# Two attention stages: TensorE turns a unit's weights ahead of the values product of the unit before it

## The chip, the cores and the metric

The program runs on one core of a Trainium2 chip. The metric is the device time of that core in microseconds, from the first to the last instruction of one launch. Three timed executions of the kernel before are given, and one more execution was taken with the hardware profiler; every row below comes from that one.

## The reference, cut to what matters

The model is a chain of six layers on a batch of 64 sequences of 128 tokens of width 128, all in fp32. Two of the six have attention with 16 heads of width 8. Only these two are touched by the change.

```python
# layer L0_xattn: cross attention, 77 context tokens, masked
scores = jnp.einsum('nhqd,nhkd->nhqk', q, k)
scores = jnp.where(mask == 0, jnp.float32(-1000000000.0), scores)
attn = jax.nn.softmax(scores / math.sqrt(dk), axis=-1)
out = jnp.einsum('nhqk,nhkd->nhqd', attn, v)
return out.transpose(0, 2, 1, 3).reshape(n, qlen, h * dk) @ wo.T + bo
...
# layer L1_xattn, first half: self attention that keeps the u = 5 largest scores of each row
scores = jnp.einsum('bhqd,bhkd->bhqk', q, k) * (1.0 / math.sqrt(D))
_, idx = jax.lax.top_k(scores, u)
...
# layer L1_xattn, second half: cross attention over the 77 context tokens, no mask, then a feed-forward part
x_cross = _mha_cross(x, memory, cross_in_w, cross_in_b, cross_out_w, cross_out_b)
h = jax.nn.gelu(x @ ffn_w1.T + ffn_b1, approximate=False)
```

## The kernel before, in words

Six stages run one after the other. The stage of L0_xattn (tiles `xa_...`) and the stage of L1_xattn (tiles `de_...`, "the decoder") share one class, `Attend`. Both work in rounds over groups of four sequences; there are 16 groups, and the rounds of different groups are laid over each other like a pipeline, so there are 19 rounds, of which the first and the last ones are partly empty. A round is one block of code for each engine, and all engines meet at a barrier between rounds.

Inside a round the attention is cut into **units**: one unit is 8 of the 16 heads of one sequence, so a sequence is two units. The xattn stage has 8 units in a round, all of the masked kind that needs no search. The decoder has 16: steps 0 to 7 are self-attention units with a search for the largest scores (`topk`), steps 8 to 15 are cross-attention units without one (`whole(t)` is true for these).

Each engine walks through the steps t = 0, 1, 2, ... of the round in its own fixed order, and semaphores tie the orders together. For a unit t without a search the chain is:

1. TensorE `pe_scores` (L1011, and L1015 for the mask) in step t-2, into banks 0 and 1.
2. VectorE `dve_shift` (L1154, L1157) in step t-1: row maximum, and scores minus maximum, into `e`.
3. ScalarE `act_exp` (L1094) in step t.
4. TensorE `pe_turn` (L1026) in step t: 8 transposes of `e` into banks 4 and 5.
5. ScalarE `act_turned` (L1100) in step t+1: copies banks 4 and 5 into `pt`.
6. TensorE `pe_values` (L1037) in step t+1: weights times values into bank 6, for the 8 heads.
7. After the second unit of a sequence: ScalarE `act_values` (L1106) copies bank 6 into `ot`, TensorE `pe_back` (L1045) turns it, VectorE `dve_normalise` (L1163, L1166) divides, TensorE `pe_out` (L1050), ScalarE `act_out` (L1111) copies into `ots`, TensorE `pe_project` (L1054), VectorE `dve_add`.

Banks 4 and 5 exist once. So `pe_turn` of unit t waits for `pt` of unit t-1, which is the same signal that `pe_values` of unit t-1 waits for:

```python
def pe_turn(self, pe, t):
    self.wait(pe, "pick" if self.topk(t) else "exp", t)
    self.wait(pe, "pt", t - 1)
...
def pe_values(self, pe, t):
    self.wait(pe, "pt", t)
```

ScalarE's order inside step t is fixed by `act_step`: `act_exp(t)`; in even steps `act_out`, which waits for `pe_out`, the last thing TensorE did in step t-1; then `act_turned(t-1)`; in even steps `act_values`, which waits for `pe_values(t-1)`, the last values product of a sequence. After `act_step` the stage adds its own work to some steps: in the xattn stage two activations after step 1, one after step 2, one after step 3, and after step 4 the query bias (L1380) and four rows of a layer norm (L881 into `xa_z`), after step 5 four more rows (into `xa_y_tok`). In the decoder, after step 8, the last two bias activations of the feed-forward part (L2358) and the Gelu (L2362, with a table load), on which TensorE's second feed-forward product (L2323) waits; that product stands between steps 8 and 9 of TensorE. After step 10 stand four rows of a layer norm (L881 into `de_xn`), which wait for GpSimd, and a copy (L2153).

Of the kernel before, what the change touches and what calls it, by code (L numbers as in the profile page):

```python
# [915 lines left out]
class Attend:  # L916
# [139 lines left out]
    def pe_step(self, pe, t):  # L1056
        there, early = self.unit(t + 2) is not None, not self.whole(t + 1)
        if there and early:
            self.pe_scores(pe, t + 2)
        if self.unit(t - 1) is not None:  # L1060
            self.pe_values(pe, t - 1)
        if t % 2 == 0 and self.unit(t - 4) is not None:
            self.pe_project(pe, (t - 4) // 2)
        if self.unit(t) is not None:
            self.pe_turn(pe, t)
        if there and not early:
            self.pe_scores(pe, t + 2)
        if t % 2 == 0 and self.unit(t - 2) is not None:
            self.pe_back(pe, (t - 2) // 2)
        if t % 2 == 1 and self.unit(t - 3) is not None:  # L1070
            self.pe_out(pe, (t - 3) // 2)
# [1755 lines left out]
```

## Time and profile before

| | us |
|---|---|
| timed executions | 8492.16, 8483.58, 8464.30 |
| median of them | 8483.58 |
| the profiled execution, its own time | 8499.55 |
| its span, first to last instruction | 8497.5 |
| xattn stage, attention at work | about 4240 to 4930 |
| decoder stage | about 6370 to 8110 |

The span and the execution's own time differ by 2 us, which lie outside of the instructions. The two stages of the change take 2430 us of the 8497. "Granted clock" is the share of full speed that TensorE was given over a stretch; at any moment it is either 2.4 GHz (1.00) or 1.2 GHz (0.50), so 0.90 over a stretch means that a fifth of it ran at the lower level.

### The profile page before, as it was taken

The numbers are of one execution on the slowest core, as the hardware profiler recorded it, in microseconds if no ns is written. First come the engines' busy times: TensorE is split into PE (matmuls) and PEld (weight loads), VectorE is DVE, ScalarE is ACT, GpSimd is POOL, SyncE is SP. The second block draws the span as 40 slices with busy tenths as digits, with TensorE's granted clock in tenths as the row PEclk, the third lists the DMA queues.
The fourth block names the chain that finished last, engine by engine and source line by source line (L and its number), as shares of the span: only waits on it lengthen the run. The fifth ranks groups of instructions, "written<-read, shape, count | busy, mean of one in ns | idle before, by whom it ended". The sixth has DMA issues, their size and how long they took to land. (4 is left out here: it accounts for less than half of the span.)

```text
span 8497.5 us, 93901 instructions
## 1 busy us (share of the span) xinstructions
PE 6487.2 (76%) x25844; PEld 3454.5 (41%) x25859; DVE 6694.5 (79%) x15635; ACT 4390.8 (52%) x8810; POOL 4876.1 (57%) x2829
## 2 busy tenths in 40 slices
PE   5888888888888888888788867777556777777745
PEld 2333333333333333333355545555434545555532
DVE  5999999999999999999755558888667666666657
ACT  3555555555555555555455523333226666666633
POOL 4888878888888878888644434444222333333310
PEclk8898889899898899898898978888658988888855
DMA  5333333334333333333300046767310000000011
GB/s 184 133 148 155 137 149 155 132 148 160 133 148 155 132 153 151 137 148 155 112 25 22 20 132 204 208 201 206 92 47 7 10 9 9 9 9 9 6 31 36
DMA packets 373728, 896.56 MB, mean 106 GB/s; under 512 B 28031, under 2 KB 270076, under 8 KB 306972
## 3 DMA queue, kind: packets, MB, share of 16 engines
q1 hardware_dynamic: 332508, 692.64, 21.7%
q0 software_dynamic: 40960, 201.36, 8.3%
q14 instruction: 208, 1.70, 0.1%
q8 instruction: 52, 0.85, 0.0%
HBM read 850.58 MB, written 56.77 MB: 107 GB/s over the span
## 5 line engine op out<-in xcount | busy, mean ns | idle before, releaser
L380 POOL TENSOR_TENSOR mb_dBu<-mb_dtu,mb_rows_b 128x1024 f32<-128x1024 f32 x1027 | 2405.7, 2359 | 363.3 <-DVE mb_bank L394 186.6
L394 DVE TENSOR_TENSOR_SCAN mb_bank<-mb_bank,mb_dBu 128x1024 f32<-128x1024 f32 x704 | 1612.8, 2291 | 72.0 <-PEq L63 50.9
L434 PE MATMUL mb_bank<-mb_hcd,ident 128*128 128x512 f32 x2560 | 1271.6, 624 | 78.9 <-DVE mb_hcd L408 78.8
L365 ACT ACTIVATE mb_bank<-mb_dt,mb_a_neg 128x508 f32<-128x508 f32 x2050 | 1315.1, 673 | 0.8
L434 PE MATMUL mb_bank<-mb_hcp,ident 128*128 128x512 f32 x1280 | 796.7, 755 | 355.0 <-POOL mb_hcp L417 355.0
L417 POOL TENSOR_TENSOR mb_hcp<-mb_hs,mb_rows_c 128x1024 f32<-128x1024 f32 x320 | 752.8, 2352 | 360.0 <-DVE mb_hs L394 359.7
L408 DVE TENSOR_TENSOR mb_hcd<-mb_bank,mb_rows_c 128x1024 f32<-128x1024 f32 x704 | 862.1, 1225 | 31.3
L434 PEld LDWEIGHTS mb_bank<-mb_hcd,ident 128*128 128x128 f32 x2560 | 502.1, 203 | 798.3 <-issue 591.3
L1537 POOL DMA_INDIRECT ex_rows<-in_ex_table,ex_idx x512 | 490.3, 958 | 561.3 <-DVE ex_idx L1533 331.9
L394 DVE TENSOR_TENSOR_SCAN mb_hs<-mb_bank,mb_dBu 128x1024 f32<-128x1024 f32 x320 | 730.9, 2284 | 42.2 <-ACT mb_bank L365 42.2
L434 PEld LDWEIGHTS mb_bank<-mb_hcp,ident 128*128 128x128 f32 x1280 | 284.8, 236 | 806.1 <-POOL mb_hcp L417 480.1
L362 ACT ACTIVATE mb_bank<-mb_zeros 128x8 f32<-128x8 f32 x1025 | 175.9, 172 | 725.9 <-DVE mb_hcd L408 351.2
L207 PE MATMUL mb_bank<-mb_h_ch,mb_w_conv 128*128 128x512 f32 x1040 | 493.7, 618 | 0.0
L1026 PE MATMUL de_bank<-ident,de_a_e 128*128 128x128 f32 (+1 forms) x2048 | 332.6, 315 | 202.3 <-DVE de_a_e L1146 202.3
L996 POOL TENSOR_TENSOR de_a_km<-de_xT,hmask 128x2048 f32<-128x2048 f32 x64 | 231.8, 3622 | 394.1 <-PE de_bank L1011 252.5
L996 POOL TENSOR_TENSOR de_a_km<-de_kT,hmask 128x1232 f32<-128x1232 f32 x64 | 157.6, 2462 | 523.0 <-PE de_bank L1011 523.0
L1026 PEld LDWEIGHTS de_bank<-ident,de_a_e 128*128 128x128 f32 (+1 forms) x2048 | 270.2, 166 | 247.5 <-DVE de_a_e L1146 226.1
L996 POOL TENSOR_TENSOR xa_a_km<-xa_kT,hmask 128x1232 f32<-128x1232 f32 x64 | 144.5, 2258 | 360.8 <-PE xa_bank L1015 262.8
L1131 DVE MAX8 de_a_m<-de_a_sp 128x8 f32<-128x128 f32 x1024 | 210.3, 280 | 154.5 <-ACT de_a_sp L1080 96.1
L1089 ACT ACTIVATE de_a_e<-de_a_sp,de_a_nb 128x128 f32<-128x128 f32 x1024 | 314.4, 402 | 32.5 <-PEq L63 32.5
L207 PEld LDWEIGHTS mb_bank<-mb_h_ch,mb_w_conv 128*128 128x128 f32 x1040 | 211.2, 203 | 281.1 <-issue 281.1
L1591 PE MATMUL ex_bank<-ex_rows,ex_dg_in 128*128 128x256 f32 x1024 | 322.7, 486 | 0.0
(369 smaller groups left out, 13327.9 us busy)
## 6 DMA issues: line engine op xcount, KB each, us to landing
mb_rows_b<-bc_rows SPq DMA_DIRECT2D x259, 1024.0 KB, 7.6
mb_rows_c<-bc_rows SPq DMA_DIRECT2D x258, 1024.0 KB, 6.8
stream<-mb_r_post SPq DMA_DIRECT2D x69, 256.0 KB, 2.4
mb_r_tok<-stream SPq DMA_DIRECT2D x67, 256.0 KB, 2.8
mb_r_post<-stream SPq DMA_DIRECT2D x65, 256.0 KB, 2.9
ex_rows<-in_ex_table,ex_idx POOLq DMA_INDIRECT x512
tj_x_tok<-stream SPq DMA_DIRECT2D x17, 256.0 KB, 3.0
bc_rows<-mb_xp SPq DMA_DIRECT2D x65, 64.0 KB, 1.6
```

The lines of the kernel that those rows point to most:

```text
L207: m = nc.tensor.matmul(bank[:, M0 + c], w_conv[:, k, c * P:(c + 1) * P], h_ch[:, :, k:k + SEQ], start=(k == 0), stop=(k == DC - 1))
L365: e = nc.scalar.activation(da_of(n)[:, c * GB:(c + 1) * GB, 1:], dt[q][:, c].rearrange("p (b t) -> p b t", b=GB)[:, :, 1:], ACT.Exp, scale ...
L380: nc.gpsimd.tensor_tensor(by_c(dBu[m % RING][:]), by_c(chains(dtu[q][:])), over_c(rows_b[:, n]), ALU.mult).then_inc(s["mb_dbu"], 1)
L394: nc.vector.tensor_tensor_scan(flat(to), flat(da_of(n)), flat(dBu[n % RING][:]), 0.0, ALU.mult, ALU.add).then_inc(s["mb_scan"], 1)
L408: nc.vector.tensor_tensor(by_c(hcd[k % 3][:]), by_c(da_of(n)), over_c(rows_c[:, n]), ALU.mult).then_inc(s["mb_hcd"], 1)
L417: nc.gpsimd.tensor_tensor(by_c(hcp[k % 2][:]), by_c(hs[k % 2][:]), over_c(rows_c[:, n]), ALU.mult).then_inc(s["mb_hcp"], 1)
L434: m = nc.tensor.matmul(bank[:, B_Y + c], ident[:], part[:, c * GB:(c + 1) * GB], start=False, stop=False)
L996: self.nc.gpsimd.tensor_tensor(self.km[n % 2][:, :, 0:nk], kind.k(n % GB).unsqueeze(1).to_broadcast([P, H, nk]), self.hmask[:].unsqueeze(2 ...
L1026: m = self.nc.tensor.transpose(self.bank[0:nk, 4 + h // 4, (h % 4) * P:(h % 4 + 1) * P], self.e_of(t, nk)[:, h], self.ident[:])
L1089: m = self.nc.scalar.activation(self.e_of(t, nk)[:, h], self.sp[t % 2][:, h, 0:nk], ACT.Exp, scale=kind.scale, bias=self.nb[:, t % 2, h:h ...
L1537: nc.gpsimd.indirect_dma_start(rowsb[b][:, h], None, w["table"], bass.IndirectOffsetOnAxis(idx[b][:, h:h + 1], 0)).then_inc(got[b], 16)
L1591: m = nc.tensor.matmul(bank[:, HID, 0:FI], dg_in[:, h], rowsb[k % GB][:, h, IB:IB + FI], start=False, stop=(h == PH - 1))
```

## The change

In `pe_step`, TensorE's order within a step, a unit without a search is turned before the values product of the unit behind it. Units with a search keep the old order. No instruction is added or removed.

```diff
         there, early = self.unit(t + 2) is not None, not self.whole(t + 1)
         if there and early:
             self.pe_scores(pe, t + 2)
+        if self.whole(t):
+            self.pe_turn(pe, t)
         if self.unit(t - 1) is not None:
             self.pe_values(pe, t - 1)
         if t % 2 == 0 and self.unit(t - 4) is not None:
             self.pe_project(pe, (t - 4) // 2)
-        if self.unit(t) is not None:
+        if self.topk(t):
             self.pe_turn(pe, t)
         if there and not early:
             self.pe_scores(pe, t + 2)
```

## Rows read from the trace of the kernel before

**Rows 1.** Stages: length, busy PE, PEld, DVE, ACT, POOL (instructions), granted clock, DMA share, GB/s.
```profile
4240.00:4930.00 690.00, 604.11 (x4540) 375.08 (x4539) 374.87 (x1169) 350.18 (x614) 272.67 (x219) 0.89 0.08 21
6370.00:8110.00 1740.00, 1273.47 (x9089) 865.17 (x9087) 1157.03 (x4988) 1096.45 (x2232) 617.65 (x385) 0.85 0.03 9
```

**Rows 2.** TensorE's waits in each stage: us in total, times, longest.
```profile
PE xa_bank L1037 <- ACT xa_a_pt L1100: 85.6, 62, 2.8
...
PE de_bank L1037 <- ACT de_a_pt L1100: 168.0, 143, 3.7
PE de_bank L2323 <- ACT de_hT L2362: 34.7, 15, 2.3
```

**Rows 3.** TensorE in order of time, xattn, steps 4 to 6 of a round.
```profile
4655.44 0.64 PE L1037 MATMUL xa_bank<-xa_a_pt,xa_vx 77*32 77x128 f32 x16
4656.01 0.49 PE L1054 MATMUL xa_bank<-xa_wo,xa_a_ots 128*128 128x128 f32 x2
4656.34 1.04 PE L1026 MATMUL xa_bank<-ident,xa_a_e 128*77 128x128 f32 x8
4657.21 0.68 PE L1011 MATMUL xa_bank<-xa_a_km,xa_qT 128*128 128x308 f32 x2
...
4660.43 0.64 PE L1037 MATMUL xa_bank<-xa_a_pt,xa_vx 77*32 77x128 f32 x16 [0.76 <-ACT xa_a_pt L1100]
...
4665.44 0.64 PE L1037 MATMUL xa_bank<-xa_a_pt,xa_vx 77*32 77x128 f32 x16 [1.37 <-ACT xa_a_pt L1100]
...
4669.60 0.64 PE L1037 MATMUL xa_bank<-xa_a_pt,xa_vx 77*32 77x128 f32 x16
```

**Rows 4.** ScalarE in order of time, the same round, steps 4 to 7.
```profile
4656.15 0.60 ACT L1106 ACTIVATE xa_a_ot<-xa_bank 128x512 f32<-128x512 f32 x1 [1.15 <-PE xa_bank L1037]
...
4657.21 1.65 ACT L881 ACTIVATE xa_z<-xa_r_tok,xa_n_shift,xa_n_rstd 128x128 f32<-128x128 f32 x4
...
4659.36 1.01 ACT L1100 ACTIVATE xa_a_pt<-xa_bank 77x1024 f32<-77x1024 f32 x1
...
4664.11 0.28 ACT L1111 ACTIVATE xa_a_ots<-xa_bank 128x128 f32<-128x128 f32 x1 [1.58 <-PE xa_bank L1050]
4664.29 1.01 ACT L1100 ACTIVATE xa_a_pt<-xa_bank 77x1024 f32<-77x1024 f32 x1
4666.14 0.60 ACT L1106 ACTIVATE xa_a_ot<-xa_bank 128x512 f32<-128x512 f32 x1 [0.84 <-PE xa_bank L1037]
...
4667.41 1.02 ACT L1100 ACTIVATE xa_a_pt<-xa_bank 77x1024 f32<-77x1024 f32 x1
```

**Rows 5.** TensorE, decoder, steps 8 and 9 of a round.
```profile
7134.94 0.64 PE L1037 MATMUL de_bank<-de_a_pt,de_vself 128*32 128x128 f32 x16
7135.84 1.04 PE L1026 MATMUL de_bank<-ident,de_a_e 128*77 128x128 f32 x8
...
7140.69 5.47 PE L2323 MATMUL de_bank<-de_w,de_hT 128*128 128x128 f32 x32 [2.33 <-ACT de_hT L2362]
```

**Rows 6.** ScalarE, decoder, the same step 8, and step 10.
```profile
7135.65 0.60 ACT L1106 ACTIVATE de_a_ot<-de_bank 128x512 f32<-128x512 f32 x1 [1.13 <-PE de_bank L1037]
...
7152.44 1.66 ACT L881 ACTIVATE de_xn<-de_a,de_n_shift,de_n_rstd 128x128 f32<-128x128 f32 x4 [0.95 <-POOL de_n_shift L875]
```

**Rows 7.** The same turn and values at the lower clock, xattn, TensorE.
```profile
4616.38 1.08 PE L1037 MATMUL xa_bank<-xa_a_pt,xa_vx 77*32 77x128 f32 x16 [1.37 <-ACT xa_a_pt L1100]
4617.98 1.91 PE L1026 MATMUL xa_bank<-ident,xa_a_e 128*77 128x128 f32 x8
```

**Rows 8.** Busy time by engine over two whole rounds of each stage, xattn first.
```profile
4605.42:4654.48 49.06, 43.35 (x290) 26.72 (x289) 24.50 (x78) 22.58 (x41) 18.43 (x16) 0.79 0.08 22
4654.48:4694.05 39.57, 34.17 (x291) 21.31 (x289) 24.10 (x78) 22.59 (x41) 18.44 (x16) 1.00 0.11 28
...
6607.04:6712.72 105.68, 77.42 (x572) 53.06 (x573) 72.52 (x314) 69.31 (x142) 39.78 (x25) 0.90 0.03 10
7140.69:7249.94 109.25, 81.16 (x573) 55.40 (x573) 72.09 (x314) 69.20 (x142) 39.74 (x25) 0.84 0.03 9
```

## The prediction

> **What bounds the kernel now.** I began with the busy time by engine in the two stages that the change touches [rows 1]. In the xattn stage TensorE is busy for 604 of 690 us, no other engine for more than 375: TensorE sets the pace, and only the 86 us in which it stands idle can be won. In the decoder it is busy for 1273 of 1740 us and VectorE for 1157; which of them waits changes within a round. Together the stages are 2430 us, so one per cent of them is 0.3% of the kernel.
>
> Next I read TensorE's waits [rows 2]. In the xattn stage one line holds practically all of the idle time: the values product (L1037) waiting for ScalarE's copy of the turned weights (L1100), 85.6 us in 62 waits. The decoder has the same wait (168 us, partly in units with a search) and one for the Gelu (L2323 waiting for L2362), 15 times 2.3 us.
>
> Then I laid TensorE's and ScalarE's order of time side by side for a few steps [rows 3, 4], to see who is late behind the copy. In step 5 TensorE waits 0.76 us and in step 6 1.37 us. In step 6 ScalarE had first to copy `ots` at 4664.11, for which it had waited 1.58 us for `pe_out` (L1050), the last thing that TensorE does in step 5; only then came the turned weights, at 4664.29. So the wait of step 6 is a round trip through `pe_out`, and the turned weights had been ready long before. In step 5 ScalarE never waited for the turn either: from `ot` at 4656.15 it ran without a gap through the query bias, four rows of the norm, the exponent and the copy, to 4660.37, and what it had waited for ahead of that (1.15 us) was the values product. The reader is to see that ScalarE's queue, not the turn, is what makes the copy late.
>
> **The change part by part.** Nothing is removed or added; one group of 8 transposes trades places with one group of 8 values products (and the projection behind it in even steps). I take the effects one by one.
>
> *The wait ahead of the pair.* Turn t and values t-1 wait for the same copy, since banks 4 and 5 exist once. The exponent of unit t stands ahead of that copy in ScalarE's order, so the turn finds it done. The pair starts when it started before: 0.
>
> *The turn ends earlier*, by the values product (4655.44 to 4656.01, 0.57 us) and in even steps the projection (0.33 us) [rows 3]. Who can use that? Only the copy of unit t. For odd t it stands behind `act_out`, which waits for the end of TensorE's step, so nothing is won. For even t it stands behind `act_values`, which waits for the values product of unit t-1; this is the very one that now comes later. So nothing is won there either. VectorE's `shift` of unit t+2 also waits for the turn, but its turn comes a step later, so it has cover. Gain: 0; the upper bound is the rival below.
>
> *The values product ends later*, by the turn: 4656.34 to 4657.21, 0.87 us at the full clock [rows 3]. Behind `act_values` ScalarE holds everything else, so the question is for each even step how much cover there is before TensorE needs what comes next.
> - Xattn, step 6: `ot` at 4666.14, the copy ends at 4668.43 and TensorE comes for it at 4669.60 [rows 3, 4]. Cover 1.17 us, need 0.87: hidden. In steps 0 and 2 TensorE has the next group's transposes besides, so the cover should be no smaller: hidden.
> - Xattn, step 4: no cover at all, since the chain runs without a gap to TensorE's 0.76 us wait. It becomes 1.63. `act_step` is in step 4 followed by both extra pieces in the rounds that have a next group and a norm two ahead, 14 of them. 14 x 0.87 = 12.2 us. TensorE's remaining steps of the round depend on ScalarE only through `pe_out`, so the delay reaches the end of the round whole.
> - Decoder, step 8: values product at 7134.94, `ot` at 7135.65 after a wait of 1.13, and behind it in ScalarE's queue two bias activations, a table load and the Gelu, on which TensorE waits 2.33 us until 7140.69 [rows 5, 6]. Again no cover. The turn there takes the same 0.87. Fifteen rounds have this wait [rows 2]: 15 x 0.87 = 13.1 us.
> - Decoder, step 10: behind `ot` ScalarE waits 0.95 us for GpSimd [rows 6], which swallows 0.87. Steps 12 and 14 have no wait of TensorE on this chain; there ScalarE also waits for other things. 0, at most 0.87 for one of them in each of 15 rounds, 13 us.
> - `pe_back` waits for `ot` but stands at the end of the same step, behind four scores products. `dve_add` waits for the projection, now 0.87 later, ahead of the `shift` that TensorE's next scores need; that `shift` has a step of slack. 0.
>
> At the lower clock the turn takes nearly twice as long (1.91 against 1.04 us busy) [rows 7], but so does everything with which TensorE covers ScalarE, whose own work does not stretch; step 4 then has cover. So the price per place lies between 0 and 0.87, or 1.6 if only the turn is slow; I take 0.87, as the step 4 and step 8 rows are at the full clock.
>
> Sum: 12.2 + 13.1 = 25.3 us more. The profiled execution took 8499.55 us, which would become 8524.9. It lies 16 us above the median of the three timed ones, 8483.58, and on that the sum gives 8508.9. I predict 8509.
>
> **The clock.** A whole xattn round took 49.06 us at a granted clock of 0.79 and the next one, with the same instructions, 39.57 us at 1.00; a decoder round took 105.68 us at 0.90 and a later one 109.25 at 0.84 [rows 8]. So the clock moves a round by far more than the 0.87 us of the change, and adding idle time of TensorE may tip it in either direction. This is the largest unknown of the forecast, and the reason for most of the range.
>
> The Trainium skill (page TensorE: Matmul & The Clock Gate, section Part 1: The HAM clock gate) says that the throttled state is the default and that activity releases it. No row here contradicts this, but the two xattn rounds differ by 9.5 us with nearly equal idle time (5.7 and 5.4 us), so the amount of idle alone does not decide it here. By that rule the added idle should cost clock, which is the second rival below, at 8537; by the rows alone the sum is 8509.
>
> **The rivals.**
> - *The delays arrive as computed*: 8509, with a range of its own of 8495 to 8523, from the scatter of the three times. Chance 0.42.
> - *More time at the lower clock.* The longer idle of steps 5 (1.63 us, followed by 1.37) and 9 (3.2 us) is followed by more work at 1.2 GHz. Price: if half of the 14 xattn rounds lose the half of the difference between the two rows of [rows 8] less often seen now, say 4 rounds x 4.7 = 19 us, and the three decoder rounds or so that still are of the short kind lose 3.6 us each, 11 us; with some of it overlapping, 28 us on top, 8537. It decides against the first case from about one xattn round in seven. Chance 0.17.
> - *The clock swallows the delays.* The rounds of the decoder repeat with one length; if they keep it, the 13.1 us vanish, and with half of the xattn part the time is 8490. It also stands for cover that I did not see. Chance 0.20.
> - *Less time at the lower clock.* A moved phase lets the decoder's long rounds become the short kind: 12 x 3.6 = 43 us less, against 25 more: 8466. It ends on the other side from 8 such rounds on. Chance 0.13.
> - *The early turn does what it says*: the waits of L1037 shrink by the values product, because ScalarE's copy is bound by the turn after all. Three such waits in each of 14 + 15 rounds, 0.57 each, 50 us less: 8434. Against it speaks the order in ScalarE's queue [rows 4]. Chance 0.08.
>
> **How the numbers follow.** About 0.3% or 25 us is what a measurement of this kernel can tell from no change. The first case lies on that bound, so I give half of it to each side. Slower by over 0.3%: 0.21 + 0.16 = 0.37. Within: 0.21 + 0.19 + 0.06 = 0.46. Faster: 0.07 + 0.08 + 0.02 = 0.17. The range leaves out the last rival and the extreme of the second: 8465 to 8545.
>
> **What would show it.** In the profile after: in 14 xattn rounds the wait ahead of step 5 grows from 0.76 to about 1.6, and now stands at L1026 instead of L1037; the wait ahead of step 6 stays 1.37; the decoder's L2323 waits 3.2 instead of 2.33; ScalarE's wait ahead of L1106 grows by 0.87 everywhere, while its wait ahead of L1100 hardly moves. A full-clock xattn round takes 40.4 instead of 39.57 us. The prediction is wrong if the 1.37 us waits shrink (then the turn was on the path), if the 0.76 does not grow (then ScalarE's chain had cover), or if the number of rounds at each clock moves the total by more than the 25 us.

## The result, and the profile after

The changed kernel takes 8607.61 us (median of 5 runs, 8599.93 to 8623.65), the kernel before 8481.15 (median of 5). The ratio is 1.0156 with a 95% interval of 1.0143 to 1.0169: 126 us slower, where 25 were forecast, and outside the range of 8465 to 8545.

The waits of TensorE in the profile after, xattn stage first (us in total, times, longest), beside [rows 2]:

```profile
PE xa_bank L1026 <- ACT xa_a_pt L1102: 101.4, 62, 2.9
...
PE de_bank L2325 <- ACT de_hT L2364: 46.8, 15, 3.2
```

The number of waits is the same, 62 and 15. The first group grew from 85.6 to 101.4 us, the second from 34.7 to 46.8. That is 15.8 and 12.1 us, 28 together, against the 12.2 and 13.1 of the forecast. In order of time TensorE goes through steps 4 to 6 of a round of the xattn stage like this, at the full clock:

```profile
4612.44 1.04 PE L1026 MATMUL xa_bank<-ident,xa_a_e 128*77 128x128 f32 x8
4613.40 0.64 PE L1037 MATMUL xa_bank<-xa_a_pt,xa_vx 77*32 77x128 f32 x16
...
4618.48 1.07 PE L1026 MATMUL xa_bank<-ident,xa_a_e 128*77 128x128 f32 x8 [1.71 <-ACT xa_a_pt L1102]
...
4623.65 1.07 PE L1026 MATMUL xa_bank<-ident,xa_a_e 128*77 128x128 f32 x8 [1.36 <-ACT xa_a_pt L1102]
```

The reader is to compare with [rows 3]: the wait ahead of step 5 is 1.71 us instead of 0.76, the one ahead of step 6 1.36 instead of 1.37, and both now stand at the turn. ScalarE in the same steps, beside [rows 4]:

```profile
4614.12 0.60 ACT L1108 ACTIVATE xa_a_ot<-xa_bank 128x512 f32<-128x512 f32 x1 [2.03 <-PE xa_bank L1037]
...
4622.32 0.28 ACT L1113 ACTIVATE xa_a_ots<-xa_bank 128x128 f32<-128x128 f32 x1 [1.85 <-PE xa_bank L1050]
```

It waits 2.03 us for the values product where it waited 1.15, which is the turn's 0.87. So far everything went as predicted. Where is the rest? In the busy time. Both stages again, with the changed kernel's longer windows (columns as in [rows 1]):

```profile
4240.00:5020.00 780.00, 677.50 (x4515) 413.21 (x4515) 373.83 (x1169) 345.19 (x614) 271.65 (x219) 0.80 0.07 19
6460.00:8230.00 1770.00, 1294.51 (x9078) 866.88 (x9076) 1149.05 (x4993) 1089.95 (x2231) 617.71 (x386) 0.86 0.03 9
```

The xattn stage takes 780 us instead of 690. TensorE is busy for 677.5 us with the same instructions that took 604.1 before: 73 us more, beside 16 us more of waiting, make up the 90. The granted clock of the stage fell from 0.89 to 0.80. VectorE's and ScalarE's busy times did not grow. In the decoder the busy time grew by 21 us and the Gelu wait by 12, in a stretch 30 us longer, although the mean clock over it did not fall (0.86 after 0.85); so its 21 us can't be put down to clock from these rows. The comparison of rounds, beside [rows 8]:

```profile
4657.22:4710.52 53.30, 46.47 (x290) 28.17 (x289) 24.37 (x78) 22.30 (x41) 18.36 (x16) 0.74 0.08 21
4710.52:4756.19 45.67, 39.14 (x290) 24.31 (x289) 24.04 (x78) 22.30 (x41) 18.36 (x16) 0.89 0.10 24
...
7143.57:7252.74 109.17, 80.50 (x573) 54.21 (x573) 71.68 (x314) 68.86 (x142) 39.73 (x25) 0.87 0.03 9
```

Before, rounds of 39.57 us at 1.00 came up again and again; after, the rounds at the highest clock are like the second row here, 45.67 us at 0.89. A decoder round of 105.7 us, as the first rounds before had it, was not found after: all 13 full rounds come at about 109.2, as the third row shows, where the trace before has nine of that length.

### The profile page after: what moved, and what is told of

It reads as the page before. It is cut to its first block and busy times, and to the rows that moved or that the text cites. A ratio compares the mean times of both kernels' runs of the same rounds, so it can differ in the third digit from the quotient of the medians.

```text
span 8621.7 us, 93901 instructions
## 1 busy us (share of the span) xinstructions
PE 6572.9 (76%) x25844; PEld 3488.8 (40%) x25859; DVE 6683.1 (78%) x15635; ACT 4370.9 (51%) x8810; POOL 4870.4 (56%) x2829
```

## The experiments

All medians are compared with executions of the kernel before on the same chip, whose own median moved between 8460.92 and 8476.83 us from group to group. I give the ratio with its interval; the us are differences of medians. Each kernel has one trace. For the xattn stage I quote the row of the stretch from 4300 to 4850 us, which lies inside the stage in every kernel; for the two orders it reads, before and after:

```profile
4300.00:4850.00 550.00, 478.88 (x3618) 296.21 (x3620) 303.85 (x961) 284.69 (x504) 232.79 (x189) 0.90 0.09 24
```

```profile
4300.00:4850.00 550.00, 476.61 (x3142) 290.48 (x3141) 265.67 (x844) 244.01 (x438) 201.18 (x165) 0.79 0.08 22
```

In the same time TensorE is busy equally long and gets through 13% fewer instructions.

The edits of the first kernels are one condition. `per` is 4 in the xattn stage and 8 in the decoder:

```diff
+        first = self.whole(t) and (CONDITION)
+        if first:
+            self.pe_turn(pe, t)
         if self.unit(t - 1) is not None:
             self.pe_values(pe, t - 1)
         if t % 2 == 0 and self.unit(t - 4) is not None:
             self.pe_project(pe, (t - 4) // 2)
-        if self.unit(t) is not None:
+        if self.unit(t) is not None and not first:
             self.pe_turn(pe, t)
```

**The two stages apart.** Condition `self.per == 4`:

> The new order in the xattn stage alone. The changed kernel lost 126 us by the medians; in the two profiles the xattn stage accounts for about 92 to 96 us of the 124 us of span. Both theories below expect 85 to 105 us more than the kernel before here, and 14 waits of 1.71 us ahead of step 5. If the loss is spread differently (a lost clock that carries over from stage to stage), it is clearly less or more than that.

8575.35 us against 8473.52, ratio 1.0119 (1.0102 to 1.0136), 102 us. As expected.

Condition `self.per == 8`:

> The new order in the decoder alone: 15 waits of 3.20 us for the Gelu in place of 2.33 (13 us). Expected 15 to 35 us more than before; decoder rounds stay at 109.2 us in most rounds, as in both profiles. Together with the xattn-only kernel it should make up the 126 us.

8516.74 us against 8473.52, ratio 1.0045 (1.0030 to 1.0059), 43 us, above the expected 35. The sum of the two is 145, a little more than the 126 of both.

**Is it the added idle?** Condition `self.per == 4 and t == 4`:

> Xattn stage, new order in step 4 alone: this adds all of the idle time of the change (0.76 to about 1.7 us ahead of step 5, 14 times), but no transposes stand directly behind a wait, since step 4 itself begins without one. Theory A (the added idle tips the clock): most of the 90 us, 60 to 100. Theory B (the turn directly behind a wait tips the clock, whatever the length of the wait): 12 us of idle and little else, 5 to 30.

8490.07 us, ratio 1.0018 (1.0006 to 1.0030), 17 us. This kernel has the whole added wait and the new order in no other step, and it costs what the sum had said within its interval. Theory A falls. The added wait is not quite free of clock, though: the stage's granted clock is 0.87, and in the trace the stage grew by 24 us, counted from the first query product (out of `xa_wq`, one in each round) to the last: 668.4 after 644.5.

Condition `self.per == 4 and t != 4`:

> Xattn stage, new order in every step but 4: the wait ahead of step 5 stays 0.76 to 0.85 us, so no idle time is added, but turns stand directly behind the waits of steps 0, 2, 5 and 6. Theory A: 0 to 15 us more than before and a granted clock of 0.89 in the stage. Theory B: 60 to 90 us more and a granted clock near 0.80.

8526.30 us, ratio 1.0053 (1.0033 to 1.0074), 53 us, with no longer wait ahead of step 5. The clock is 0.85. Theory B is nearer, but 17 and 53 make 70 of the 102 us.

**Which steps?** Condition `self.per == 4 and t in (1, 3, 7)`, the steps without a wait:

> Xattn stage, new order in steps 1, 3 and 7 alone, where TensorE comes to the pair without a wait. Theory B3 (it matters whether the turn or the values product stands directly behind a wait): 0 to 8 us more than before, rounds of 39.6 us and longer ones mixed as before. If it costs 25 us or more, the place behind a wait is not what matters in the kernel with every step but 4 (53 us more).

8495.64 us against 8476.83, ratio 1.0023 (1.0011 to 1.0034), 19 us; more than the 8 that I allowed, less than 25. The clock is 0.89 after 0.90.

Condition `self.per == 4 and t in (0, 2, 5, 6)`, the steps that begin with one:

> Xattn stage, new order in steps 0, 2, 5 and 6 alone, each of which begins with a wait; the length of the waits changes by less than 0.15 us. Theory B3: 35 to 60 us more than before, rounds near 46 us and none of 39.6. Theory C (a matter of the rounds' phase against the clock alone): anything between -20 and +60.

8558.85 us, ratio 1.0108 (1.0075 to 1.0141), 82 us by the medians. This was more than expected, and almost the loss of the whole change in this stage. Its waits and its stage row:

```profile
PE xa_bank L1026 <- ACT xa_a_pt L1103: 65.2, 45, 2.9
```

```profile
4300.00:4850.00 550.00, 486.04 (x3201) 293.61 (x3202) 270.02 (x853) 247.54 (x444) 205.40 (x168) 0.79 0.08 22
```

45 waits of 1.45 us in the mean; the kernel before has, over the same stretch, 51 waits of 1.39 us. So the length of the waits is the same, the work is the same, and the clock is 0.79 instead of 0.90. Only the order of turn and values product behind the wait differs.

This kernel also spoils the simple account that the turn behind a wait is what costs. The kernel above with every step but 4 is this one with the new order in steps 1, 3 and 7 on top. Those steps alone cost 19 us, so it should cost about 100; it costs 53, and the intervals of the two kernels (1.0033 to 1.0074, 1.0075 to 1.0141) do not meet. In the traces this kernel settles at rounds of about 51.1 us, and the one with more of the new order in it at 46.0:

```profile
4679.69:4730.78 51.09, 45.43 (x291) 27.30 (x289) 24.54 (x78) 22.30 (x41) 18.38 (x16) 0.77 0.08 22
```

```profile
4673.87:4719.89 46.02, 40.36 (x290) 24.91 (x289) 24.26 (x78) 22.30 (x41) 18.35 (x16) 0.85 0.10 24
```

So the cost is not a property of a step that can be added up.

**Work put into the waits.** If idle time of TensorE is what lets the clock fall, filling it must bring the clock back, whatever the order. The fill goes into columns of bank 6 that a later values product overwrites, ahead of the waits of steps 0, 2, 5 and 6:

```diff
+    def fill():
+        for k in range(2):
+            nc.tensor.matmul(bank[:, 6, 384:512], ident[:], ident[:], start=True, stop=True)
...
     for t in range(8):
+        if t in (0, 2, 5, 6) and has_now and (t or has_ended):
+            fill()
         at.pe_step(pe, t)
```

> New order in the xattn stage alone (102 us more than before without a fill), plus two ordinary 128x128 products of the unit matrix with itself, about 0.65 us at the full clock, into unused columns of bank 6 ahead of the waits of steps 0, 2, 5 and 6; they fit inside the waits and their values are never read. Theory B1 (the clock follows TensorE's work other than turns): the stage gets most of its clock back, 0 to 50 us more than before. Theory B2 (any TensorE work counts alike): the same here, so it is the next kernel that tells them apart. Theory C (the clock follows neither, only the phase of the rounds): still about 100 us.

8470.32 us against 8460.92, ratio 1.0013 (1.0001 to 1.0024): 9 us above the kernel before without a fill, where it was 102. Clock 0.92.

With six `nc.tensor.transpose` in place of the two products:

> As the kernel with the matmul fill, but the fill is six turns of the unit matrix, also about 0.65 us. B1 (turns do not count as activity): no relief, 85 to 115 us more than before. B2 (any work counts): relief as with the products, 0 to 50 us.

8454.97 us against 8460.92, ratio 0.9982 (0.9969 to 0.9995), 6 us less than before by the medians. The stage row:

```profile
4300.00:4850.00 550.00, 503.88 (x4044) 323.32 (x4045) 305.88 (x986) 287.65 (x516) 236.68 (x192) 0.97 0.09 24
```

B1 falls: turns bring the clock back too, and B2 stands in that both kinds count. Which of the two kinds does more can't be read from this pair, because the fills are not equally long: in the traces the two products are four instructions of 0.61 us together, the six turns are six of 0.82 us, and the wait left behind them is 0.93 us in the mean with products and 0.68 with turns. Theory C falls, as far as it said that the fill would not help.

The product fill in the old order:

> The kernel before with the product fill in the same four places of the xattn stage. If idle time of TensorE is what loses the clock in the old order too, the stage's granted clock rises from 0.89 to 0.95 or more and the time falls by 15 to 50 us: rounds of 39.6 us instead of 43.9 on average would be 60 us. If not, 0 to 5 us more.

8432.15 us, ratio 0.9962 (0.9951 to 0.9974), 29 us less. Clock 0.92. The old order, too, lost clock to its waits. Compared with this kernel, and not with the one without a fill, the new order still costs 38 us when both have the products.

The turn fill in the old order:

> The kernel before with six turns of the unit matrix in each of the four waits of the xattn stage, the fill that brought the new order from 102 us above to about 15 us below. If the loss of the new order is its 12 us of idle plus clock and nothing else, the old order with the same fill is 12 to 15 us faster than the new one with it: 25 to 40 us less than before, granted clock 0.95 or more. If the two orders with this fill are equal, the 0.87 us ahead of step 5 is hidden by something.

8441.55 us against 8468.68, ratio 0.9969 (0.9955 to 0.9983). The new order with the same fill has 0.9982. The difference is 0.13% or 11 us, inside the sum of the two intervals but equal to the 12 us of idle that the new order adds. The clock did not reach the 0.95 that I expected, it is 0.93. With the turn fill the two orders are worth what the sum of the prediction said; with the product fill they are 38 us apart, without one 102. The mean clock does not rank the filled kernels: the new order with turns has the highest, 0.97, and is slower than both of the old order, with 0.93 and 0.92. The clock of a row counts TensorE's idle time too, and in the old order there is less of it: 516.3 of 550 us busy here against 503.9, since the turns take the place of two of the four waits (26 are left in the stretch, where there were 51).

**Which kind of work behind the wait?** Here I had a theory that would have closed the case: that the values product, 16 short passes on 32 columns of the array, counts for more than the turn, so that it must stand directly behind the wait. Both kernels start from the order in steps 0, 2, 5 and 6. The first issues the values product one more time ahead of the turn (`False` leaves out its signal):

```diff
         if first:
+            if self.unit(t - 1) is not None:
+                self.wait(pe, "exp", t)
+                self.pe_values(pe, t - 1, False)
             self.pe_turn(pe, t)
```

> The kernel with the new order in steps 0, 2, 5 and 6 of the xattn stage (about 92 us more than before), with the values product issued an extra time directly behind the wait, ahead of the turn; its result is overwritten by the same numbers. It is 0.57 us of extra work in each of four places, 14 or 15 rounds, 33 us in all. If it is the kind of work directly behind the wait that decides the clock (the values product is counted as more activity than the turn), the granted clock of the stage returns to about 0.90 and the total is 30 to 60 us more than before. If it is only a matter of phase, or of how long TensorE works between waits, the clock stays near 0.8 and the total is 100 us or more above before.

8527.67 us against 8475.68, ratio 1.0055 (1.0037 to 1.0072), 52 us; the clock is 0.89. Less 33 us for the extra work, 19 are left of 82. It fits the theory. The second turns five of the eight heads one more time, `for h in [*range(5), *range(HH)]`:

> The same, but with five of the eight turns issued an extra time directly behind the wait: the same 0.55 to 0.6 us of extra work, of the other kind. Kind-of-work theory: no return of the clock, 110 to 140 us more than before. Length-of-work theory: like the kernel with the values product twice.

8485.68 us, ratio 1.0014 (1.0004 to 1.0024), 10 us, extra work and all. The stage row, and TensorE's waits in the same stretch:

```profile
4300.00:4850.00 550.00, 478.22 (x3818) 305.85 (x3818) 295.46 (x947) 278.13 (x501) 229.78 (x187) 0.96 0.09 24
```

```profile
PE xa_bank L1026 <- ACT xa_a_pt L1103: 71.8, 50, 2.9
```

The waits are as long as ever (1.44 us), and the clock is 0.96. I had expected 110 to 140 us. The theory falls, with its sign: five more turns (0.55 us) bring more clock than one more values product (0.57 us) does. What the two have in common is that TensorE works longer between one wait and the next; that this is what helps is a reading, not shown.

**The decoder.** The fill ahead of the wait for the Gelu, on top of the new order in the decoder alone:

```diff
 if t == 8 and has_ffn:
+    for k in range(18 if has_cross else 0):
+        nc.tensor.transpose(bank[:, 6, 384:512], ident[:], ident[:])
     pe.wait_ge(p["gelu"], 1)
```

> New order in the decoder alone (43 us more than before without a fill), plus 18 turns of the unit matrix into unused columns ahead of the 3.2 us wait for the Gelu: about 2 us of work inside the wait, 15 times. If the clock answers to idle time as in the xattn stage, the decoder rounds leave the 109.2 us and the time falls to 0 to 30 us more than before. If the rounds are held at 109.2 us by something else, 35 to 50 us more.

8515.56 us against 8476.83, ratio 1.0047 (1.0035 to 1.0058): no gain over 1.0045. The wait shrank from 3.2 to 1.2 us and the rounds kept their length to a tenth of a microsecond, at a granted clock of 0.88:

```profile
7134.19:7243.42 109.23, 82.17 (x590) 56.51 (x590) 71.72 (x314) 69.04 (x142) 39.79 (x25) 0.88 0.03 9
```

Condition `self.per == 8 and t == 8`:

> Decoder, new order in step 8 alone: all of the added wait for the Gelu (2.33 to 3.20 us, 15 times, 13 us) and no turn behind a wait. If the decoder is like the xattn stage, 8 to 20 us more than before, with rounds of 104 to 109 us mixed as before. If the longer wait alone holds the rounds at 109.2 us, 30 to 50 us more.

8484.43 us against 8475.68, ratio 1.0011 (0.9999 to 1.0023), 9 us, not told from 0. The longer wait does not hold the rounds at 109.2 either: not one of the 13 full rounds has that length, and there are rounds like this one, of 106.11 us.

```profile
7141.59:7247.70 106.11, 79.19 (x573) 54.02 (x573) 71.81 (x314) 69.26 (x142) 39.85 (x25) 0.87 0.03 9
```

Condition `self.per == 8 and t != 8`:

> Decoder, new order in steps 9 to 15 alone: no added wait for the Gelu, turns directly behind the waits of steps 10 to 15. Place-behind-the-wait theory: 20 to 40 us more than before, rounds held at 109.2 us. Added-idle theory: 0 to 10 us more.

8492.20 us, ratio 1.0010 (0.9998 to 1.0022), about 9 us by the ratio and 17 by the medians, not told from 0 either. In its trace six of the 13 rounds take 109.2 us. Neither half does alone what both do together, 9 and 9 to 17 against 38 to 43, though the intervals leave room for a plain sum.

The rounds of all the traces say more on the decoder than those of the profiles before and after. Fourteen of these kernels leave the decoder as it was, and in their traces it has two to eight rounds of 109.2 us and takes 1500 to 1521 us from the first to the last of its 16 second feed-forward products. The kernel with the new order in the xattn stage alone has three such rounds:

```profile
6713.01:8213.27 1500.26, 1095.26 (x8032) 752.12 (x8032) 989.64 (x4226) 960.50 (x1929) 552.04 (x356) 0.88 0.03 9
```

The trace before, with nine and 1524 us, is at the long end. The three kernels with the whole new order in the decoder have 13 of 13, and 1547, 1547 and, with the fill, 1543 us. So by these traces the cost in the decoder is that every full round is of the long kind. And the unedited decoder differs by up to 24 us between kernels that were edited in an earlier stage only; whether the edit does that, or one execution against the next, no run here shows.

**Taking the waits away.** In [rows 4] ScalarE's copy waits for `pe_out`, which stands behind the scores for no reason of data. And ScalarE has idle time at the end of the round for the norm that makes step 5 late:

```diff
+        ahead = self.per == 4 and t in (1, 5)
+        if ahead and self.unit(t - 3) is not None:
+            self.pe_out(pe, (t - 3) // 2)
         if there and not early:
             self.pe_scores(pe, t + 2)
...
-        if t % 2 == 1 and self.unit(t - 3) is not None:
+        if t % 2 == 1 and not ahead and self.unit(t - 3) is not None:
             self.pe_out(pe, (t - 3) // 2)
...
-                        if t == 4 and has_norms:
+                        if t == 6 and has_norms:
                             n1.act(act, r_tok[here], z1)
...
-                        if t == 6 and has_norms:
+                        if t == 7 and has_norms:
                             pool.wait_ge(p["n1_rows"], 1)
```

> The kernel before with two edits in the xattn stage that take the waits away rather than moving them: pe_out ahead of the scores in steps 1 and 5, so that ScalarE is through act_out and the copy while TensorE makes scores, and the norm's four rows after step 6 instead of after step 4 (with GpSimd's use of them in step 7). The waits of steps 2, 5 and 6 (0.75, 0.76, 1.37 us) vanish in 14 rounds: 40 us less by the waits alone; with less idle time before the turns the clock should gain too, so 40 to 90 us less than before. If only the phase of the rounds decides the clock, 20 to 40 us less.

8390.08 us against 8460.92, ratio 0.9913 (0.9887 to 0.9938), 71 us less. This is the fastest kernel of the study. TensorE's waits in the same stretch went from 71.1 us in 51 to

```profile
PE xa_bank L1037 <- ACT xa_a_pt L1103: 41.3, 29, 2.8
```

and its order of time shows steps 4, 5 and 6 without a wait, where there were 0.76 and 1.37 us, and a new one of 0.18 us ahead of step 7:

```profile
4369.85 0.64 PE L1037 MATMUL xa_bank<-xa_a_pt,xa_vx 77*32 77x128 f32 x16
...
4374.02 0.64 PE L1037 MATMUL xa_bank<-xa_a_pt,xa_vx 77*32 77x128 f32 x16
...
4377.44 0.65 PE L1037 MATMUL xa_bank<-xa_a_pt,xa_vx 77*32 77x128 f32 x16
...
4381.85 0.65 PE L1037 MATMUL xa_bank<-xa_a_pt,xa_vx 77*32 77x128 f32 x16 [0.18 <-ACT xa_a_pt L1103]
```

The new order on top of it, in the xattn stage:

> The kernel with pe_out early and the norm late (about 75 us less than before), with the new order in the xattn stage on top. With nearly no waits left there is nothing for the new order to lengthen and hardly an idle stretch that a turn could follow: within 20 us of the kernel without it, so 50 to 90 us less than before. If the new order costs clock by itself, waits or not, 0 to 40 us less than before.

8453.15 us against 8476.83, ratio 0.9981 (0.9966 to 0.9996). It gives 0.7% of the 0.9% back, with a clock of 0.90 after 0.93. I had expected the order not to matter any more; it still does. In part it brings waits back: over the same stretch they are 52.8 us in 39 after 41.3 in 29, with 2.92 us ahead of step 0, 0.18 ahead of step 5 and 1.14 ahead of step 7, where it was 0.18.

The turn fill ahead of steps 0 and 2, in the old order:

> The kernel with pe_out early and the norm late, plus the turn fill ahead of the waits of steps 0 and 2, the only waits left. The stage still ran at 0.93 without it; at 0.98 it gains 15 to 25 us more: 85 to 100 us less than before. If the first waits are not what loses the rest of the clock, the same as without the fill within 10 us.

8404.11 us against 8468.68, ratio 0.9926 (0.9909 to 0.9942): not different from the 0.9913 without the fill. The clock rose from 0.93 to 0.95, and the time did not follow. The wait of step 2 was gone already without the fill, so half of the fill is plain extra work.

## Why the prediction was wrong

**What held.** The wait ahead of the pair starts when it did, the early turn helps nobody, and the late values product costs its 0.87 us in exactly the two places named. Predicted 1.63 us ahead of step 5, measured 1.71; 1.37 ahead of step 6, measured 1.36; 3.20 for the Gelu, measured 3.20. 12.2 us of idle in the xattn stage, measured 15.8, the rest of it 0.08 to 0.09 us more at three of the four waits of a round (0.84 after 0.75 ahead of step 2, 2.92 after 2.83 ahead of step 0, and the 1.71), which the sum had at 0; 13.1 in the decoder, measured 12.1. The kernels with only the added wait cost 17 us (step 4, xattn) and 9 us (step 8, decoder), as the sum says within their intervals. The rival in which the early turn shortens the waits falls: the 1.37 us waits did not move.

**The step that failed** is the paragraph on the clock. It saw that "the clock moves a round by far more than the 0.87 us of the change" and then put 0 into the sum for it, and 28 us into the rival "more time at the lower clock", with a chance of 0.17. Measured, the rival had the right sign and neither the size nor the cause: the clock is worth 73 of the 126 us in the xattn stage alone, as longer busy time of the same instructions at 0.80 after 0.89. The rival's cause, the longer idle, cost 17 us and not 102 when it stood alone. The last of the prediction's own signs of being wrong, that the rounds at each clock move the total by more than 25 us, is the one that came true. The sign was the one that the Trainium skill's rule (page TensorE: Matmul & The Clock Gate, section Part 1: The HAM clock gate) gives, that activity releases the throttle. The trace agrees as to fills, which raised the granted clock in every kernel of the xattn stage that had one.

Three things were wrong in its sizing. I took the clock as a response to added idle only. The added idle alone (step 4) cost 17 us; the turn behind the wait in steps 0, 2, 5 and 6, with no wait longer, cost 82. And I took the short xattn rounds of [rows 8] as one kind among several that would mostly stay; after the change not one is left. And the price was cut on the way: "half of the 14 xattn rounds" is seven, 33 us at 4.7 each, and the sum went on with four, 19 us.

**The cause, as far as it is shown.** The loss of the xattn stage is 16 us of waiting and 73 us of granted clock. The clock comes back when TensorE works in or directly behind the waits: 102 us above the kernel before become 9 with products in them, and 6 below it with turns. With the turn fill the orders differ by 11 us, the added idle, so there beside clock and idle no third loss is needed; with the shorter product fill 38 us between the orders remain. That the clock is lost in the steps that begin with a wait is only partly borne out: the new order in those alone cost 82 us, and in three more steps 53. The loss of the decoder is seen, as long rounds throughout, and not explained.

**What stays open.** Why TensorE gets less clock for wait, turn, values, scores than for wait, values, turn, scores, with equal waits and equal work. It is not that the values product counts for more than the turn; the kernels that issue each of them again say the opposite. Moving the turn changes two neighbourhoods at once, what stands behind the wait and what stands ahead of the scores, and no run here separates these in the steps with a wait. For the decoder it is open why its rounds come at 109.2 us with a clock of 0.84 before and 0.86 to 0.88 after, why the whole new order leaves no other length while its halves do, and why a fill of 2 us does not change that. The clock falls and rises in stretches, so the rounds of a loop settle into a pattern with it, and parts of a change do not add up: step 4 with 17 us and the others with 53 give 102, while of those others steps 1, 3 and 7 with 19 and the rest with 82 give 53. That last sentence is a reading of the sums, not a thing that a run isolated.

## What to carry to other kernels

An order of work on TensorE that leaves every wait as long as it was can still cost a tenth of its clock (0.79 after 0.90 here); so for a change to an engine that runs near its full clock with short waits in it, compare the granted clock by round before pricing the waits, and give the clock its own term and not only a rival. Where a wait of about a microsecond is left on TensorE, take it away first (here `pe_out` ahead of the scores and a norm moved to where ScalarE is idle, 0.87%), and if it can't be taken away, try a few useless turns or products in it (0.31% and 0.38% here); on top of the first remedy the fill gave nothing more. Compare by time and not by the mean clock alone, and compare a filled kernel with the old order filled as well. And the early turn helped nobody because ScalarE had other work queued ahead of the copy that needs it: read the consumer's queue, not only the data flow.

## What the runs showed of the hardware

- With four waits of 0.8 to 2.9 us in a round of 44 to 50 us, the xattn stage had 0.90 of the clock in the old order and 0.79 in the new one. Six fp32 turns at each of them, 0.82 us, raised that to 0.93 and 0.97.
- Turns hold the clock. The Trainium skill (page TensorE: Matmul & The Clock Gate, section Part 4: PE-mode transpose) says that a transpose doesn't count as TensorE being busy in the same way. The runs here differ: with turns as the fill the stage of the new order had 0.97 after 0.79, with the shorter fill of products 0.92; with five extra turns behind each wait it had 0.96, and with an extra values product of the same length 0.89.
- An xattn round of the same 290 TensorE instructions took 39.6 us at a clock of 1.00 (before) and 53.3 us at 0.74 (after), and TensorE's idle time in them, 5.4 and 6.8 us, makes up 1.4 of the 13.7 us between them.
- Rounds of the decoder repeat at 109.2 us to within 0.1 us for many rounds, in kernels whose work and waits differ by 1 to 2 us a round. With the unedited decoder, two to nine of 13 rounds had this length, kernel by kernel.
